# Edge softmax of a graph layer: keys loaded earlier, run marks made ahead of the scores, carries applied by two operations, differences written in place

## The chip, the cores and the metric

One core of a Trainium2 chip runs one program. The metric is device time in microseconds (us) of an execution, given as the median of three. Engines are named as the profile does: PE (TensorE) multiplies and transposes, PEld is its weight load, DVE (VectorE), ACT (ScalarE) and POOL (GpSimd) compute, SP (SyncE) starts transfers. POOL also starts the indirect DMAs, which gather one row for each of 128 indices. DMAs started by SP form one queue.

## What is computed

A residual block of 2500 tokens with 512 features: a graph attention over 80000 edges, a slice attention and a mixture of experts. Only the edge part matters here. For each of 8 heads, with `src` and `dst` the ends of an edge:

```python
diff = hr_dst - hr_src
score = s_src + s_dst + einsum(diff, a_dif) + einsum(abs(diff), a_abs) + einsum(hr_src * hr_dst, a_prd)
alpha = leaky_relu(score, 0.2)
m = segment_max(alpha, src)
ex = exp(alpha - m[src])
att = ex / (segment_sum(ex, src)[src] + 1e-16)
out = segment_sum(att * h_e[dst], src)
```

## The kernel before

The edges are sorted by source, padded, and cut into 336 groups of two tiles of 128 edges (5376 edges to a piece, 16 pieces). `program` (L1887) runs phase after phase; each phase is a block, and no engine enters the next one before all have left the last. The phases around the change are these.

`score_edges` (L970). For each group POOL gathers 2 tiles of target rows (520 floats a row) into one of six buffers `rows_v` (L1047). PE expands the source rows with a one-hot matrix into `ps_u` (L1111), which has a single buffer and so serves the two tiles of a group in turn. DVE subtracts (`w<-rows_v,ps_u`, L1073), PE transposes `w` (L1126), ACT takes magnitudes and slopes (L1157, L1164), DVE multiplies them (L1086), PE adds over the features of a head and adds a term read from `w` itself (L1135, L1138), ACT copies the scores out (L1170) and SP writes them to DRAM in four parts (L1031). The semaphore `differed` counts subtracted tiles, `summed` counts groups through L1138. The order on each engine is written out by `in_turns`: in step n an engine does each of its operations for group n minus a fixed distance, the first 12 and the last steps unrolled, the others in a loop with semaphore values computed in registers. PE's order in step n is expand tile 0 of n-2, one-hot of n-1, heads of n-6, expand tile 1 of n-2, transpose n-3. DVE's is tile 0 of n-2, multiply n-5, tile 1 of n-2, one-hot of n (L1065). POOL is unrolled.

`softmax_weights` (L1175). SP loads the four parts of the scores, each 2.7 MB as 128 rows (8 heads by 16 pieces) of 5376 columns, and then the sorted records for each head in three DMAs (`keys`, L1211 to L1213). DVE makes `reset`: 0 where the source stays the same, -1e38 where a run of equal sources ends (L1229 to L1231). It adds the four parts (L1233 to L1235), applies leaky relu (L1236), and takes the maximum within each run by a scan from the left and one from the right (L1239, L1240). The ends of each piece go through DRAM to 8 rows, are scanned over the 16 pieces and come back as a carry for each row (L1216 to L1222, L1248 to L1252). Then both scans run again with the carries as start values, and the larger of the two is subtracted from `alpha`. ACT takes exp of all 5376 columns, and 42 times PE transposes 128 columns (L1273) and ACT copies them to `weights` (L1265), with two PSUM buffers in turn.

`gather_messages` (L1276). DVE zeroes `denominators` and `sums` (L1320, L1321). POOL gathers two tiles of message rows for each group into six buffers (L1313), DVE makes one-hots (L1327) and multiplies rows by weights (L1331, two SBUF inputs), PE sums (L1355, L1356), and DVE adds these sums up (L1341, L1343).

Of the kernel before, what the change touches and what calls it, by code (L numbers as in the profile page):

```python
# [14 lines left out]
P = 128  # L15
# [954 lines left out]
def score_edges(nc, a, const, edge, group_block, tab_v, parts, parts_in, scores):  # L970
# [13 lines left out]
    with ExitStack() as ctx:  # L984
# [14 lines left out]
        w, w_abs = [sb(f"w{q}", [P, GROUP, EW]) for q in range(TURN)], sbs("w_abs", [P, KF, GE])  # L999
# [22 lines left out]
        def _(sp):  # L1022
            for tile, part in ((a_abs, 3), (minus_prd, 4)):
                for h in range(HEADS):
                    sp.dma_start(tile[h * R:(h + 1) * R, :], a["L0_gnn_a"][h, part * D:(part + 1) * D].rearrange("(c r) -> r c", r=R),
                                 allow_slow_non_contiguous=True).then_inc(vectors_in, 16)
            with nc.sync.Fori(0, GROUPS // BUFS) as t:
# [10 lines left out]
        def _(pool):  # L1038
            nc.gpsimd.iota(head_i[:, :], pattern=[[1, 1]], base=0, channel_multiplier=1).then_inc(iota_set, 1)

            for n in range(GROUPS):
                q = n % TURN
                if n >= TURN:
                    pool.wait_ge(differed, (n - TURN + 1) * GROUP)
# [6 lines left out]
        def _(dve):  # L1051
# [123 lines left out]
def softmax_weights(nc, const, scores, merged, carry, weights, from_left):  # L1175
# [6 lines left out]
    with ExitStack() as ctx:  # L1182
# [6 lines left out]
        keys = sb("keys", [P, PIECE + 2], I32)  # L1189
        reset = sb("reset", [P, PIECE + 1])  # L1190
        alpha, from_right = sb("alpha", [P, PIECE]), sb("from_right", [P, PIECE])
# [5 lines left out]
        ps_t = [ctx.enter_context(nc.psum_tensor(f"ps_weight_t{h}", [P, 512], F32)) for h in range(2)]  # L1197
        keys_in, scores_in = sem("keys_in"), sem("scores_in")
# [7 lines left out]
        def _(sp):  # L1206
            for k, part in enumerate(score_parts):
                sp.dma_start(part, scores[k * HEADS:(k + 1) * HEADS, :].rearrange("h (c x) -> (h c) x", c=CHUNKS)).then_inc(scores_in, 16)
            for h in range(HEADS):
                rows = slice(h * CHUNKS, (h + 1) * CHUNKS)  # L1210
                sp.dma_start(keys[rows, 1:PIECE + 1], merged[1:1 + EP, :].rearrange("(c x) o -> c (x o)", c=CHUNKS)).then_inc(keys_in, 16)  # L1211
                sp.dma_start(keys[rows, 0:1], merged[0:EP, :].rearrange("(c x) o -> c (x o)", c=CHUNKS)[:, 0:1], allow_slow_non_contiguous=True).then_inc(keys_in, 16)
                sp.dma_start(keys[rows, PIECE + 1:PIECE + 2],  # L1213
                             merged[2:2 + EP, :].rearrange("(c x) o -> c (x o)", c=CHUNKS)[:, PIECE - 1:PIECE], allow_slow_non_contiguous=True).then_inc(keys_in, 16)
# [734 lines left out]
```

## Time and profile before

| what | us |
|---|---|
| three executions, median (lowest to highest) | 3604.73 (3603.67 to 3625.55) |
| the profiled execution | 3586.76 |
| its span, by the trace | 3584.8 |
| busy in the span: PE, DVE, POOL, ACT | 2740.9, 2248.0, 1651.8, 1448.0 |

The profile is of one execution. Times in the rows are microseconds from the start of its span; a duration ahead of the word "mean" is in ns. The clock of PE is given as a share of full speed, 0.50 being 1.2 GHz and 1.00 being 2.4 GHz. "a <-b" after idle time names what ended it. In a row of the timeline the first number is the start and the second the time to the end of the last instruction merged into it.

### The profile page before, as it was taken

To read this page: it belongs to the slowest core of one execution; us is meant where nothing else is said; L and a number is where in the kernel's file an instruction comes from. 1 tells how busy PE (TensorE), PEld (TensorE's weight loads), DVE (VectorE), ACT (ScalarE), POOL (GpSimd) and SP (SyncE) were. 2 spreads that over 40 slices of the span, in tenths; PEclk is the share of its full clock that TensorE was granted. 3 is DMA by queue.
4 is the path that set the end of the run, shared out by engine and by line. 5 is a ranking of instruction groups with operands and counts; after the bars stand their busy time and mean duration, and the time that the engine had idled before them with its cause. 6 is when DMAs were issued, how large, how long until landed. Compare 5 with 4: busy or idle time off the path is not lost. (4 is left out here: it accounts for less than half of the span.)

```text
span 3584.8 us, 65271 instructions
## 1 busy us (share of the span) xinstructions
PE 2740.9 (76%) x17311; PEld 1764.0 (49%) x17312; DVE 2248.0 (63%) x4027; ACT 1448.0 (40%) x2941; POOL 1651.8 (46%) x1562
## 2 busy tenths in 40 slices
PE   2599887989999989989991057777777777779892
PEld 2366544666666666666661034444444444477440
DVE  3667635777777777777772967777777777742111
ACT  1233315888888888888882010000000000033220
POOL 1133204444444444444440047777777777612112
PEclk9799988999999999999996579999999999959996
DMA  3012134555555555555555035666666665641124
GB/s 115 18 61 63 56 110 124 143 142 144 142 142 144 143 142 144 143 142 144 143 136 157 0 101 165 173 175 172 174 174 174 173 174 174 164 138 48 62 77 134
DMA packets 181565, 461.62 MB, mean 129 GB/s; under 512 B 50534, under 2 KB 66338, under 8 KB 180739
## 3 DMA queue, kind: packets, MB, share of 16 engines
q0 software_dynamic: 116400, 372.54, 37.2%
q1 hardware_dynamic: 55105, 83.86, 7.5%
q10 hardware_dynamic: 10002, 4.53, 0.5%
q8 instruction: 26, 0.43, 0.1%
q14 instruction: 32, 0.26, 0.0%
HBM read 413.88 MB, written 46.86 MB: 129 GB/s over the span
## 5 line engine op out<-in xcount | busy, mean ns | idle before, releaser
L1313 POOL DMA_INDIRECT rows_e<-message_rows,edge_dst x672 | 809.8, 1205 | 431.6 <-ACTq L1286 222.9
L1047 POOL DMA_INDIRECT rows_v<-target_rows,edge_dst x672 | 639.0, 951 | 684.0 <-DVE w L1073 577.1
L1355 PE MATMUL ps_sum<-messages,node_onehot 128*125 128x512 f32 x1344 | 745.9, 643 | 243.6 <-DVE messages L1331 154.9
L1073 DVE TENSOR_TENSOR w<-rows_v,ps_u 128x520 f32<-128x520 f32 x672 | 468.0, 696 | 376.1 <-issue 284.4
L1164 ACT ACTIVATE slope<-w_abs,a_abs,minus_prd 128x256 f32<-128x256 f32 x1344 | 697.8, 593 | 0.1
L1111 PE MATMUL ps_u<-edge_space,source_onehot_t 125*128 x4032 | 593.6, 280 | 133.5 <-DVE w L1073 131.0
L1331 DVE TENSOR_TENSOR messages<-rows_e,edge_space 128x1024 f32<-128x1024 f32 x336 | 411.6, 1225 | 246.9 <-DMA rows_e<-message_rows,edge_dst 246.5
L1111 PEld LDWEIGHTS ps_u<-edge_space,source_onehot_t 125*128 125x128 bf16 x4032 | 362.9, 97 | 357.8 <-issue 279.0
L1356 PEld LDWEIGHTS ps_den<-edge_space,node_onehot 128*125 128x125 f32 x1344 | 254.5, 189 | 329.3 <-issue 329.3
L1678 ACT COPY gate_t<-ps_count 128x32 f32<-128x32 f32 x1 | 0.2, 186 | 1030.6 <-PE ps_count L1611 1030.6
L1086 DVE TENSOR_TENSOR slope<-w_abs,slope 128x1024 f32<-128x1024 f32 x336 | 409.4, 1218 | 4.2 <-ACT slope L1164 4.2
L1126 PE MATMUL ps_w<-ident,w 128*128 128x128 f32 x2688 | 349.7, 273 | 0.0
L1157 ACT ACTIVATE w_abs<-ps_w 128x1024 f32<-128x1024 f32 x336 | 342.7, 1020 | 4.1 <-PE ps_w L1126 4.0
L1355 PEld LDWEIGHTS ps_sum<-messages,node_onehot 128*125 128x125 f32 x1344 | 200.6, 189 | 272.0 <-issue 153.2
L1126 PEld LDWEIGHTS ps_w<-ident,w 128*128 128x128 f32 x2688 | 305.6, 141 | 5.0 <-issue 0.2
L1341 DVE TENSOR_TENSOR edge_space<-ps_sum,edge_space 125x512 f32 x336 | 229.9, 684 | 20.2 <-PE ps_den L1356 12.1
L1135 PE MATMUL ps_heads<-slope,head_sum 128*32 128x256 f32 x2688 | 215.5, 392 | 4.8 <-ACT score L1170 4.8
L1151 ACT COPY source_onehot_t<-ps_onehot 125x256 bf16<-125x256 bf16 x336 | 125.1, 372 | 198.5 <-issue 140.4
L1356 PE MATMUL ps_den<-edge_space,node_onehot 128*125 (+1 forms) x1344 | 190.0, 214 | 0.0
L1273 PE MATMUL ps_weight_t<-ident,alpha 128*128 128x128 f32 x42 | 14.5, 448 | 176.8 <-ACT alpha L1261 174.0
L1065 DVE TENSOR_SCALAR source_onehot<-iota_row_bf,edge_local 128x125 bf16<-128x125 bf16 x672 | 139.0, 252 | 0.1
L1327 DVE TENSOR_TENSOR node_onehot<-iota_row,edge_local 128x250 f32<-128x250 f32 x336 | 138.2, 411 | 0.1
(380 smaller groups left out, 2943.9 us busy)
## 6 DMA issues: line engine op xcount, KB each, us to landing
scores<-score SPq DMA_DIRECT2D x1344, 8.0 KB
edge_space<-in_L_ffn_w_dram SPq DMA_DIRECT2D x24, 512.0 KB, 4.7
rows_v<-target_rows,edge_dst POOLq DMA_INDIRECT x672
rows_e<-message_rows,edge_dst POOLq DMA_INDIRECT x672
source_parts<-edge_space SPq DMA_DIRECT2D x20, 380.9 KB
edge_space<-source_parts SPq DMA_DIRECT2D x4, 1904.3 KB
token_rows_out<-token_y SPq DMA_DIRECT2D x27, 256.0 KB, 2.7
edge_space<-scores SPq DMA_DIRECT2D x2, 2688.0 KB, 28.2
```

What stands on the lines that cost most here:

```text
L1047: nc.gpsimd.indirect_dma_start(rows[q][:, j, :], None, tab_v, bass.IndirectOffsetOnAxis(ap=edge["dst"][:, tile:tile + 1], axis=0)).then_in ...
L1073: v.tensor_tensor(w[q][:, j, :].rearrange("p (a b) -> p a b", a=2), rows[q][:, j, :].rearrange("p (a b) -> p a b", a=2), ps_u[:, :, 0:HALF ...
L1086: v.tensor_tensor(slope[h][:, :, :], w_abs[h][:, :, :], slope[h][:, :, :], ALU.mult).then_inc(z_set, 1)
L1111: ins = nc.tensor.matmul(ps_u[:, half, 0:HALF], onehot_t[q % BUFS][:, j, :], rows_of_part, start=part == 0, stop=part == PARTS - 1)
L1126: ins = nc.tensor.transpose(ps_w[q % 2][:, c, j * P:(j + 1) * P], w[q][:, j, c * P:(c + 1) * P], ident[:, :])
L1157: sc.activation(w_abs[h][:, :, :], ps_w[q % 2][:, :, :], ACT.Abs).then_inc(abs_set, 1)
L1164: ins = sc.activation(slope[h][:, c, :], w_abs[h][:, c, :], ACT.Identity, bias=a_abs[:, c:c + 1], scale=minus_prd[:, c:c + 1])
L1313: nc.gpsimd.indirect_dma_start(rows[q][:, j, :], None, tab_e, bass.IndirectOffsetOnAxis(ap=edge["dst"][:, tile:tile + 1], axis=0)).then_in ...
L1331: v.tensor_tensor(messages[h][:, :, :].rearrange("p j (h d) -> p (j h) d", d=D), rows[q][:, :, :].rearrange("p j (h d) -> p (j h) d", d=D) ...
L1341: v.tensor_tensor(total, ps_sum[q % BUFS][:, :], total, ALU.add)
L1355: nc.tensor.matmul(ps_sum[h][:, :], onehot[h][:, j, :], messages[h][:, j, :], start=j == 0, stop=j == GROUP - 1)
L1356: ins = nc.tensor.matmul(ps_den[h][:, 0:HEADS], onehot[h][:, j, :], tile_weights[:, DS(n * GROUP + j, 1), :].rearrange("p o h -> p (o h)") ...
```

## The change

The `keys` tile is made outside the two phases, its 24 loads are issued by SP at the start of `score_edges`, and `w` becomes another name for `rows_v`: DVE writes the difference over the gathered row. So POOL waits for `summed` of the group six before instead of `differed`, and DVE's wait on `summed` in `differ` goes. In `softmax_weights` the run marks are made without waiting for scores, and two further scans over them (`in_first`, `in_last`, the latter in bf16) mark the columns that lie in the first and the last run of a piece. The parts of the scores are added one after another, each on its own semaphore. After the carries, instead of two scans, one maximum and one subtraction over the whole width, there are three operations on each of three stretches of 2048, 2048 and 1280 columns. ACT starts on the first stretch while DVE does the next. Transposes and copies go by four. The zeroing of `denominators` and `sums` moves to DVE's stream of `softmax_weights`.

```diff
-        w, w_abs = [sb(f"w{q}", [P, GROUP, EW]) for q in range(TURN)], sbs("w_abs", [P, KF, GE])
+        w, w_abs = rows, sbs("w_abs", [P, KF, GE])
@@ score_edges, sync, ahead of the loop
+            for h in range(HEADS):
+                rows_of_head = slice(h * CHUNKS, (h + 1) * CHUNKS)
+                sp.dma_start(keys[rows_of_head, 1:PIECE + 1], merged[1:1 + EP, :].rearrange("(c x) o -> c (x o)", c=CHUNKS)).then_inc(keys_in, 16)
...
@@ score_edges, gpsimd
-                    pool.wait_ge(differed, (n - TURN + 1) * GROUP)
+                    pool.wait_ge(summed, n - TURN + 1)
@@ score_edges, vector, differ
                     at_least(dve, gathered[q], turn * (16 * GROUP) + 16 * GROUP)
-                    at_least(dve, summed, n - TURN + 1)
@@ softmax_weights, vector
             dve.wait_ge(keys_in, 16 * 3 * HEADS)
+            v.memset(lowest[:, :], -BIG)
             link(v.tensor_scalar(keys[:, :], keys[:, :], KEY.bit_length() - 1, None, ALU.logical_shift_right))
             link(v.tensor_tensor(reset[:, :], keys[:, 1:PIECE + 2], keys[:, 0:PIECE + 1], ALU.not_equal))
             link(v.tensor_scalar(reset[:, :], reset[:, :], -BIG, None, ALU.mult))
-            dve.wait_ge(scores_in, 16 * KF)
...
+            floor = lowest[:, 0:1].broadcast_to([P, PIECE])
+            v.tensor_tensor_scan(in_first, reset[:, 0:PIECE], floor, 0.0, ALU.add, ALU.max)
+            link(v.tensor_tensor_scan(in_last[:, ::-1], reset[:, 1:PIECE + 1][:, ::-1], floor, 0.0, ALU.add, ALU.max))
+            v.tensor_copy(ends[:, 2:3], in_first[:, PIECE - 1:PIECE])
+            v.tensor_copy(ends[:, 3:4], in_last[:, 0:1])
+            for k in range(1, KF):
+                dve.wait_ge(scores_in[0], 16)
+                dve.wait_ge(scores_in[k], 16)
+                link(v.tensor_tensor(score_parts[0], score_parts[0], score_parts[k], ALU.add))
...
-            v.tensor_reduce(ends[:, 2:3], reset[:, 0:PIECE], AX.X, ALU.min)
-            v.tensor_reduce(ends[:, 3:4], reset[:, 1:PIECE + 1], AX.X, ALU.min).then_inc(ends_set, 1)
+            dve.sem_inc(ends_set, 1)
+            link(v.tensor_tensor(from_right[:, :], from_left[:, :], from_right[:, :], ALU.max))
             dve.wait_ge(pieces_in, 16)
...
+            v.memset(denominators[:, :, :], 0.0)
             dve.wait_ge(carry_in, 16)
-            scans(carry_p[:, 0:1], carry_p[:, 1:2])
-            link(v.tensor_tensor(from_left[:, :], from_left[:, :], from_right[:, :], ALU.max))
-            v.tensor_tensor(alpha[:, :], alpha[:, :], from_left[:, :], ALU.subtract).then_inc(shifted, 1)
+            for begin, end in stretches:
+                at = slice(begin, end)
+                link(v.scalar_tensor_tensor(from_right[:, at], in_first[:, at], carry_p[:, 0:1], from_right[:, at], ALU.add, ALU.max))
+                link(v.scalar_tensor_tensor(from_right[:, at], in_last[:, at], carry_p[:, 1:2], from_right[:, at], ALU.add, ALU.max))
+                v.tensor_tensor(alpha[:, at], alpha[:, at], from_right[:, at], ALU.subtract).then_inc(shifted, 1)
+            v.memset(sums[:, :, :], 0.0)
@@ softmax_weights, scalar
+            for n, (begin, end) in enumerate(stretches):
+                act.wait_ge(shifted, n + 1)
+                nc.scalar.activation(alpha[:, begin:end], alpha[:, begin:end], ACT.Exp).then_inc(exped, 1)
+                for b, (i, size) in enumerate(batches):
+                    if begin <= i * P < end:
+                        act.wait_ge(turned[b % 2], b // 2 + 1)
+                        for x in range(size):
+                            ins = nc.scalar.copy(weights[:, :, i + x, :], ps_t[b % 2][:, x, :].rearrange("p (h c) -> p c h", h=HEADS))
+                        ins.then_inc(kept[b % 2], 1)
@@ gather_messages, vector
-            v.memset(denominators[:, :, :], 0.0)
-            link(v.memset(sums[:, :, :], 0.0))
```

## Rows read from the trace of the kernel before

**Rows 1.** Two stretches: us, busy of each engine (instructions), PEclk, DMA share, GB/s.
```profile
1908.20:1961.10 52.90, 0.00 (x0) 0.00 (x0) 0.00 (x0) 0.00 (x0) 0.00 (x0) 0.50 0.93 261
1961.10:2096.40 135.30, 14.48 (x42) 7.60 (x42) 103.58 (x23) 14.77 (x43) 0.00 (x0) 0.50 0.00 0
```

**Rows 2.** Timeline of SP and DVE at the loads: start, us, engine, line.
```profile
1908.16 0.37 SPq L1208 DMA_DIRECT2D alpha<-scores  x1
...
1961.12 2.96 DVE L1229 TENSOR_SCALAR keys<-keys 128x5378 int32<-128x5378 int32 x1 [59.24 <-DMA keys<-sorted_records]
1964.12 5.76 DVE L1230 TENSOR_TENSOR reset<-keys 128x5377 f32<-128x5377 int32 x1
```

**Rows 3.** Timeline of DVE: scans, ends of pieces, carries.
```profile
1995.95 11.36 DVE L1239 TENSOR_TENSOR_SCAN edge_space<-reset,alpha 128x5376 f32<-128x5376 f32 x1
2007.23 11.33 DVE L1240 TENSOR_TENSOR_SCAN from_right<-reset,alpha 128x5376 f32<-128x5376 f32 x1
...
2034.05 0.18 DVE L1248 TENSOR_TENSOR_SCAN state<-pieces 8x16 f32<-8x16 f32 x1 [3.92 <-DMA pieces<-carry]
...
2039.31 11.42 DVE L1239 TENSOR_TENSOR_SCAN edge_space<-reset,carry_p,alpha 128x5376 f32<-128x5376 f32 x1 [4.67 <-DMA carry_p<-carry]
```

**Rows 4.** Groups of instructions, 2078 to 2096: count, busy us, mean ns, idle before.
```profile
L1273 PE MATMUL ps_weight_t<-ident,alpha 128*128 128x128 f32 x42 | 14.5, 448 | 176.8 <-ACT alpha L1261 174.0
L1261 ACT ACTIVATE alpha<-alpha 128x5376 f32<-128x5376 f32 x1 | 4.7, 4682 | 168.8 <-DVE alpha L1256 168.8
```

**Rows 5.** Timeline at the change of phase to `gather_messages`.
```profile
2095.53 0.48 ACT L1265 COPY edge_space<-ps_weight_t 128x128 f32<-128x128 f32 x2 [0.35 <-PE ps_weight_t L1273]
...
2096.93 0.95 POOL L1313 DMA_INDIRECT rows_e<-message_rows,edge_dst  x1 [222.86 <-ACTq L1286]
...
2098.66 8.59 DVE L1321 MEMSET edge_space<- 125x10240 f32 x1 [2.08 <-issue]
```

**Rows 6.** Stretch in which only the key loads run; columns as in rows 1.
```profile
1936.00:1958.00 22.00, 0.00 (x0) 0.00 (x0) 0.00 (x0) 0.00 (x0) 0.00 (x0) 0.50 0.95 113
```

**Rows 7.** Timeline of the loop of `score_edges`, one step and two later.
```profile
1102.08 0.70 DVE L1073 TENSOR_TENSOR w<-rows_v,ps_u 128x520 f32<-128x520 f32 x1 [0.89 <-issue]
...
1102.57 0.39 PE L1138 MATMUL ps_heads<-ident,w 128*8 128x128 f32 x4
...
1102.69 1.22 DVE L1086 TENSOR_TENSOR slope<-w_abs,slope 128x1024 f32<-128x1024 f32 x1
...
1109.85 0.69 DVE L1073 TENSOR_TENSOR w<-rows_v,ps_u 128x520 f32<-128x520 f32 x1 [0.77 <-issue]
```

**Rows 8.** Timeline of PE: eight transposes at 1.2 GHz in `score_edges`.
```profile
573.49 1.91 PE L1126 MATMUL ps_w<-ident,w 128*128 128x128 f32 x8
```

**Rows 9.** Section 5 of the page: count, busy us, mean ns, idle before.
```profile
L1313 POOL DMA_INDIRECT rows_e<-message_rows,edge_dst x672 | 809.8, 1205 | 431.6 <-ACTq L1286 222.9
```

**Rows 10.** Timeline of POOL in `gather_messages`, in three places.
```profile
2125.26 1.92 POOL L1313 DMA_INDIRECT rows_e<-message_rows,edge_dst  x1 [0.30 <-issue]
...
2502.26 0.95 POOL L1313 DMA_INDIRECT rows_e<-message_rows,edge_dst  x1 [0.30 <-issue]
...
3113.60 1.86 POOL L1313 DMA_INDIRECT rows_e<-message_rows,edge_dst  x1 [0.30 <-issue]
```

**Rows 11.** Timeline of DVE in the same three places.
```profile
2125.13 1.23 DVE L1331 TENSOR_TENSOR messages<-rows_e,edge_space 128x1024 f32<-128x1024 f32 x1
...
2129.67 1.23 DVE L1331 TENSOR_TENSOR messages<-rows_e,edge_space 128x1024 f32<-128x1024 f32 x1 [2.31 <-DMA rows_e<-message_rows,edge_dst]
...
2505.96 1.23 DVE L1331 TENSOR_TENSOR messages<-rows_e,edge_space 128x1024 f32<-128x1024 f32 x1 [0.86 <-DMA rows_e<-message_rows,edge_dst]
...
3119.78 1.23 DVE L1331 TENSOR_TENSOR messages<-rows_e,edge_space 128x1024 f32<-128x1024 f32 x1 [0.93 <-DMA rows_e<-message_rows,edge_dst]
```

**Rows 12.** Timeline of POOL and DVE in `write_result`.
```profile
3522.69 1.19 POOL L1869 DMA_INDIRECT back<-token_rows_out,token_slot  x1 [0.30 <-issue]
...
3528.75 1.29 DVE L1876 TENSOR_TENSOR x_sb<-x_sb,back 125x512 f32<-125x512 f32 x2 [1.61 <-DMA back<-token_rows_out,token_slot]
```

More of the change, by code:

```diff
@@ L967, in sort_and_project, with score_edges @@
         clear_semaphores(nc, sems)
-def score_edges(nc, a, const, edge, group_block, tab_v, parts, parts_in, scores):
+def score_edges(nc, a, const, edge, group_block, tab_v, parts, parts_in, scores, merged, keys, keys_in):
     ident, identb, row, rowb = const["ident"], const["identb"], const["row"], const["rowb"]
@@ L1172, in _, with softmax_weights @@
             in_turns(sc, TURNS, ((4, magnitudes), (1, keep_onehot), (4, slopes), (6, keep_scores)), TURN)
-def softmax_weights(nc, const, scores, merged, carry, weights, from_left):
+def softmax_weights(nc, const, scores, keys, keys_in, carry, weights, from_left, sums, denominators):
     with ExitStack() as ctx:
@@ L1207, in _ @@
             for k, part in enumerate(score_parts):
[L1208 to L1214, printed above, removed]
+                sp.dma_start(part, scores[k * HEADS:(k + 1) * HEADS, :].rearrange("h (c x) -> (h c) x", c=CHUNKS)).then_inc(scores_in[k], 16)
             sp.wait_ge(ends_set, 1)
@@ L1258, in _ @@
+            v.memset(sums[:, :, :], 0.0)
         @block.scalar
         def _(act):
-            act.wait_ge(shifted, 1)
-            nc.scalar.activation(alpha[:, :], alpha[:, :], ACT.Exp).then_inc(exped, 1)
-            for i in range(PT):
-                act.wait_ge(turned[i % 2], i // 2 + 1)
-                nc.scalar.copy(weights[:, :, i, :], ps_t[i % 2][:, 0:P].rearrange("p (h c) -> p c h", h=HEADS)).then_inc(kept[i % 2], 1)
+            for n, (begin, end) in enumerate(stretches):
[7 more added lines that the diff above has]
+                        ins.then_inc(kept[b % 2], 1)
@@ L1267, in _ @@
         @block.tensor
         def _(pe):
-            pe.wait_ge(exped, 1)
-            for i in range(PT):
-                if i >= 2:
-                    pe.wait_ge(kept[i % 2], i // 2)
-                nc.tensor.transpose(ps_t[i % 2][:, 0:P], alpha[:, i * P:(i + 1) * P], const["ident"][:, :]).then_inc(turned[i % 2], 1)
+            for b, (i, size) in enumerate(batches):
+                pe.wait_ge(exped, i // STRETCH + 1)
+                if b >= 2:
+                    pe.wait_ge(kept[b % 2], b // 2)
+                for x in range(size):
+                    ins = nc.tensor.transpose(ps_t[b % 2][:, x, :], alpha[:, (i + x) * P:(i + x + 1) * P], const["ident"][:, :])
+                ins.then_inc(turned[b % 2], 1)
@@ L1916, in program @@
         sums = sums_space[0:L, :].rearrange("p (b f) -> p b f", b=NB)
-        score_edges(nc, a, const, edge, group_block, tab_v, parts, parts_in, scores)
-        softmax_weights(nc, const, scores, merged, carry, weights, sums_space[:, 0:PIECE])
+        keys_in = sem("keys_in")
+        with nc.sbuf_tensor("keys", [P, PIECE + 2], I32) as keys:
+            score_edges(nc, a, const, edge, group_block, tab_v, parts, parts_in, scores, merged, keys, keys_in)
+            softmax_weights(nc, const, scores, keys, keys_in, carry, weights, sums_space[:, 0:PIECE], sums, denominators)
         gather_messages(nc, const, edge, group_block, weights, tab_e, sums, denominators)
```

28 lines of the change are left out of this document (16 added, 12 removed).

## The prediction

> **What bounds the kernel now.** I read the busy time by stage first. Between the scores and the message gathers the kernel has 188 us in which no two engines work at a time. For 52.9 us no engine computes and the DMA engines are 0.93 busy; for the next 135.3 us they are still, and DVE is busy for 103.6 us [rows 1]. The timeline says what is late there. SP issues its 28 loads from 1908.16 on and DVE starts at 1961.12, when the keys have landed [rows 2]. Then DVE does one full-width operation after another, with two waits for carries of 3.92 and 4.67 us [rows 3]. Last come 4.7 us of exp and 42 transposes [rows 4]. The last copy ends at 2096.01, so the stretch from the first load takes 187.9 us. Everything in it is on the path, since no engine enters a phase before all have left the last. That is the stretch the change rewrites; the loop of the scores, which it also touches, must be looked at for harm.
>
> **Softmax stretch after the change, from 1908.2.** Full-width operations keep their measured times; the start-to-start distance is 0.03 us more than the duration where DVE waits for itself [rows 2].
>
> Marks: the keys are in SBUF long before, so DVE can start at once. I add 1.0 us for code that may not be there yet (bounds 0 and 2.08, the unexplained idle of DVE at the next change of phase [rows 5]). Two operations of 2.96 (L1229, and L1231 of the same size), one of 5.76 [rows 2], the two new scans at the price of those there (11.3 and 11.4 [rows 3]) and small ones: 34.7 us, to 1943.9. A bf16 output has no row here; I take the price of f32 and see no reason for more. The scores are 10.75 MB and land by about 1936, the key traffic alone being what follows [rows 6]. So these marks hide the score loads and the adds wait for nothing.
>
> Scores: three adds and leaky relu, four times 5.79, then two scans and two copies, 22.9: 46.1 us, to 1990.0. The two reductions over the full width are gone.
>
> Carries: DVE does the maximum, 5.8 us, while the ends travel (3.92 [rows 3]), so that wait is hidden and the maximum shows: 1995.8. The small scans take 0.6, the way back 4.67 [rows 3]: 2001.1.
>
> Stretches: a line through DVE's 1.22 us for 1024 columns [rows 7] and 5.76 for 5376 [rows 2] gives 2.29 us for 2048 and 1.49 for 1280. Nine operations: 6.9 + 6.9 + 4.5 = 18.3 us, with `shifted` at 2008.0, 2014.9 and 2019.4. Zeroing `sums` follows, 8.6 us [rows 5], and ends at 2028.0.
>
> ACT and PE: exp of 2048 columns is 4.68 x 2048 / 5376 = 1.8 to 1.9 us [rows 4]. A transpose now comes every 0.41 us, because each waits for a copy [rows 4]. In fours, back to back, it is 1.91 / 8 = 0.24 us at the same 1.2 GHz [rows 8], and four copies are some 0.9 us (0.48 for two [rows 5]). With two buffers that makes 1.1 us for four and 5.4 us for a stretch of 16. ACT: 2008.0 + 1.9 + 5.5 = 2015.4, + 1.9 + 5.5 = 2022.8, + 1.2 + 3.6 = 2027.6. If the cadence stays 0.41 it ends at 2032. So the stretch ends at 2028.0, a gain of 68 us; 64 at the slow cadence, 69 without the 1.0 us.
>
> **Gathers after it.** POOL starts 0.9 us into the phase in both [rows 5]. The 8.6 us of zeroing are worth little there: POOL sets the pace of this phase, (809.8 + 431.6 - 222.9) / 336 = 3.03 us a group [rows 9], and had all that time been gathering ahead. DVE's first product can come 0.95 + 0.30 + 0.95 + 2.8 = 5.0 us after POOL's start instead of 10.7; I take 2 us of these 5.7 (bounds 0 and 6).
>
> **Score loop: gathers released later.** POOL's gather of group n waited for the subtraction of n-6, in step n-4, and now waits for L1138 of n-6, in step n, while DVE needs the rows in step n+2. The product of the wait is a window. L1138 ends at 1102.96; the subtraction two steps on starts at 1109.85 [rows 7], 6.9 us later. Needed: 0.3 to wake, two gathers of 0.95 with 0.30 between, and the landing. For the landing I take `gather_messages`, the same 128 rows of about 2 KB: POOL ends its second gather at 2503.21 and DVE, waiting for just that, starts at 2505.96, 2.75 us [rows 10, 11]. 310 groups of that phase wait for a landing; the first of them shows 2129.67 - 2127.18 = 2.49, the last 3119.78 - 3115.46 = 4.32, and by my reading half lie under 2.73 and all but a few under 3.4. That makes a need of 5.3 us. Added to it: the first gather would now start at 1103.25, under the multiply, which runs to 1103.91 [rows 7]. In `gather_messages` a gather that starts at 2125.26, under a product from 2125.13 to 2126.35, takes 1.92 instead of 0.95 and ends 0.83 after the product [rows 10, 11]. So it ends at 1104.73 and the need is 5.8 to 5.9 us: about 1.0 us are left over and the later release costs nothing. What hides it is that window; every microsecond of landing beyond it is paid once in three steps (release, gather, subtraction, next L1138 run over three), 0.33 us x 324 = 108 us.
>
> The Trainium skill ("SBUF — State Buffer", section "SBUF: two separate sides") speaks against this change here: a DVE operation with two SBUF inputs and a GpSimd operation that reads SBUF share a port pair as an exclusive lock, and the second to start blocks until the first ends. By that rule the first gather waits under the multiply, as the 1.92 us row has it; without it the window would have 1.7 us to spare instead of 1.0. The trace agrees with the rule for the product; for this multiply no row shows it.
>
> DVE loses one wait in the subtraction, with its register operations. DVE is idle 0.77 to 0.89 before that subtraction [rows 7] and the wait lies inside that time, so I take nothing. No row prices one wait; as the far bound I take a tenth of that idle time, 0.08 us, in 324 steps: 26 us.
>
> **Keys at the start of the scores.** 24 issues, each some 0.4 us like the first score load [rows 2], end near 570 and SP's first score write comes at 587, so SP's queue is free. The loads hold the DMA engines at 0.95 for 22 us at 113 GB/s [rows 6], beside the first twelve gathers. Groups are needed only every 4 us and are gathered over 10 us ahead. I take 1 us, bounds 0 and 11 (half of 22).
>
> **Sum.** 68 + 2 - 1 = 69 us. Against the profiled execution: 3586.8 - 69 = 3517.8. The median of the runs lies 18 us above that execution: 3604.7 - 69 = 3535.7, say 3536.
>
> **Rivals.**
> *The gathers come late* (slower). Landing in the score loop is longer than where I read it. In `write_result` POOL ends a gather at 3523.88 and DVE starts at 3528.75, 4.87 us [rows 12]; there it competes with SP's writes, as it would here with score writes of 32 KB a group. Against: the phase with the same rows shows 2.75, and score writes are few. At 4.87 the excess is 4.87 - 2.75 - 1.0 = 1.1 us, 1.1 x 108 = 119 us: 3655. It outweighs the gain from a landing of 2.75 + 1.0 + 69 / 108 = 4.4 us on. Chance 0.08, and 0.04 for a landing of about 4.0, which costs 27 us: 3563.
> *The wait on DVE was on the path.* For it: that idle time is put to issue, not to PE [rows 7]. Against: its length. 3536 - 26 = 3510. Chance 0.06.
> *Keys crowd the first gathers.* For it: the engines are nearly full with them. Against: the lead of the gathers. 3546. Chance 0.10.
> *The overlap gives nothing*, ACT and PE keep their cadence and start stalls for code: 3536 + 4 + 1 = 3541. Chance 0.12.
> The forecast itself: 0.55, with its own range 3526 to 3548; some 0.05 is left for drift between runs (they span 22 us).
>
> **Numbers.** 3536, range 3515 to 3563. One per cent, 36 us, is about what a measurement of this kernel can tell from no change. Faster by more than that means below 3568.7: all cases but the late landing at its dearer end and part of the drift, 0.88. Within 1%: a landing near 4.4, 0.06. Slower: 0.06.
>
> **What would show it.** DVE starts the marks within 3 us of SP's first score load and shows no wait for scores; softmax from first load to last copy or zeroing 120 us (124 at most); the message phase unchanged at 3.03 us a group. In the score loop POOL's first gather of a pair takes longer than 0.95, and DVE does not wait for `rows_v`; a step stays at 3.95 us. I am wrong if a step grows, if DVE's idle before the subtraction is put to the DMA, or if the span to the first score load moves by more than 10 us.

## The result, and the profile after

| | before | after |
|---|---|---|
| executions | 4 | 4 |
| median us (lowest to highest) | 3613.85 (3603.67 to 3625.55) | 3441.64 (3426.19 to 3460.44) |
| ratio, 95% interval | | 0.9525 (0.9452 to 0.9598) |
| profiled execution | 3586.76 | 3456.42 |

The kernel gained 172 us where 69 were forecast: the time lies far below the range (3515 to 3563). By phase, each cut at the starts of instructions: "scores" from POOL's first gather to SP's first score load, "softmax" to POOL's first message gather, "messages" to the last product of message rows.

| profiled execution | scores | softmax | messages | rest | mean score step |
|---|---|---|---|---|---|
| before | 1356.3 | 188.8 | 1022.9 | 465.0 | 3.95 |
| after | 1255.3 | 122.3 | 1053.1 | 471.5 | 3.63 |

The softmax stretch gained 66.5 us, as worked out. The scores gained 101.0, which no term of the sum had. The messages lost 30.2, the phases after them 6.5 and those ahead of the scores 0.5. That makes the 130.3 between the two profiled executions; before's lay 18 to 27 us under the median of its runs and after's 15 above, hence 172 between the medians.

The softmax stretch of after, cut at the end of the marks, of the two scans and at POOL's first gather (us, busy of each engine with its instructions, PEclk, DMA share, GB/s), which answers to [rows 1]:

```profile
1807.60:1842.30 34.70, 0.00 (x0) 0.00 (x0) 34.44 (x9) 0.00 (x0) 0.00 (x0) 0.50 0.76 317
1842.30:1888.40 46.10, 0.00 (x0) 0.00 (x0) 45.82 (x10) 0.00 (x0) 0.00 (x0) 0.50 0.00 0
1888.40:1929.90 41.50, 9.18 (x42) 6.91 (x42) 33.90 (x18) 12.96 (x45) 0.00 (x0) 0.58 0.01 1
```

DVE is busy for 114.2 of 122.3 us: the stretch is now one engine's work. Its timeline (start, us, engine, line):

```profile
1807.72 2.96 DVE L1235 TENSOR_SCALAR keys<-keys 128x5378 int32<-128x5378 int32 x1
...
1830.78 11.33 DVE L1240 TENSOR_TENSOR_SCAN in_last<-reset,lowest 128x5376 bf16<-128x5376 f32 x1
...
1842.28 5.75 DVE L1246 TENSOR_TENSOR alpha<-alpha,from_right 128x5376 f32<-128x5376 f32 x1
...
1888.45 5.76 DVE L1253 TENSOR_TENSOR from_right<-edge_space,from_right 128x5376 f32<-128x5376 f32 x1 [0.16 <-DVE ends L1251]
...
1899.71 2.35 DVE L1264 SCALAR_TENSOR_TENSOR from_right<-keys,carry_p,from_right 128x2048 f32<-128x2048 f32 x1 [4.71 <-DMA carry_p<-carry]
...
1916.84 1.49 DVE L1266 TENSOR_TENSOR alpha<-alpha,from_right 128x1280 f32<-128x1280 f32 x1
1920.41 8.59 DVE L1267 MEMSET edge_space<- 125x10240 f32 x1 [2.08 <-issue]
...
1934.85 1.22 DVE L1344 TENSOR_TENSOR messages<-rows_e,edge_space 128x1024 f32<-128x1024 f32 x1 [5.12 <-DMA rows_e<-message_rows,edge_dst]
```

DVE starts 0.07 us after SP's first load and never waits for a score part; the wait for the pieces is covered by the maximum (L1253), and what stays is the way of the carries, 4.71, as in [rows 3]. ACT's exps and its last copies, and POOL's first gather:

```profile
1906.81 1.91 ACT L1273 ACTIVATE alpha<-alpha 128x2048 f32<-128x2048 f32 x1 [102.48 <-DVE alpha L1266]
...
1920.20 1.35 ACT L1273 ACTIVATE alpha<-alpha 128x1280 f32<-128x1280 f32 x1
1922.30 2.05 ACT L1278 COPY edge_space<-ps_weight_t 128x128 f32<-128x128 f32 x10 [0.75 <-PE ps_weight_t L1288]
...
1929.91 0.94 POOL L1329 DMA_INDIRECT rows_e<-message_rows,edge_dst  x1 [142.80 <-ACTq L1302]
```

ACT ends at 1924.35, DVE's zeroing at 1929.00 and sets the end. Now the score loop, one step of after (DVE and POOL), which answers to [rows 7]:

```profile
1100.93 1.22 DVE L1092 TENSOR_TENSOR slope<-w_abs,slope 128x1024 f32<-128x1024 f32 x1
1102.06 0.69 DVE L1079 TENSOR_TENSOR rows_v<-rows_v,ps_u 128x520 f32<-128x520 f32 x1
...
1101.50 1.46 POOL L1054 DMA_INDIRECT rows_v<-target_rows,edge_dst  x1 [0.87 <-PE ps_heads L1144]
1103.27 0.94 POOL L1054 DMA_INDIRECT rows_v<-target_rows,edge_dst  x1 [0.30 <-issue]
```

And the rows of before that I had in hand and did not put beside each other, around the multiply at 1102.69 of [rows 7]; in brackets stands the idle time ahead of an operation and what the profile says ended it:

```profile
1101.14 0.95 POOL L1047 DMA_INDIRECT rows_v<-target_rows,edge_dst  x1 [1.78 <-DVE w L1073]
1102.39 0.94 POOL L1047 DMA_INDIRECT rows_v<-target_rows,edge_dst  x1 [0.30 <-issue]
...
1104.12 0.70 DVE L1073 TENSOR_TENSOR w<-rows_v,ps_u 128x520 f32<-128x520 f32 x1 [0.21 <-PE ps_u L1111]
```

In after the second subtraction starts at 1102.06, 0.09 before the multiply's recorded end (1100.93 + 1.22 = 1102.15). In before it starts at 1104.12, 0.21 after that end (1103.91), and the second gather of the pair had begun 0.30 us ahead of the multiply. Over the loop the gap from the multiply's end to the next subtraction is +0.22 us in before and -0.08 in after; the other distances of the chain are nearly the same (first subtraction to multiply 0.61 in both, second subtraction to the next first one 1.90 and 1.88). So 0.30 us a step, times 324 steps, 97 us of the 101, sits in that one gap. Each multiply's record reads 1.22 us in either kernel.

### The profile page after: what moved, and what is told of

It reads as the page before. It is cut to its first block and busy times, and to the rows that moved or that the text cites. A ratio compares the mean times of both kernels' runs of the same rounds, so it can differ in the third digit from the quotient of the medians.

```text
span 3454.5 us, 65133 instructions
## 1 busy us (share of the span) xinstructions
PE 2751.6 (80%) x17311; PEld 1771.4 (51%) x17312; DVE 2219.3 (64%) x4036; ACT 1443.4 (42%) x2943; POOL 1809.3 (52%) x1562
## 5 line engine op out<-in xcount | busy, mean ns | idle before, releaser
L1054 POOL DMA_INDIRECT rows_v<-target_rows,edge_dst x672 | 802.5, 1194 | 433.0 <-PE ps_heads L1144 328.4
L1368 PE MATMUL ps_sum<-messages,node_onehot 128*125 128x512 f32 x1344 | 764.0, 659 | 267.4 <-DVE messages L1344 140.9
L1079 DVE TENSOR_TENSOR rows_v<-rows_v,ps_u 128x520 f32<-128x520 f32 x672 | 466.1, 694 | 300.5 <-PE ps_u L1117 288.3
L1132 PE MATMUL ps_w<-ident,rows_v 128*128 128x128 f32 x2688 | 349.7, 273 | 0.0
L1132 PEld LDWEIGHTS ps_w<-ident,rows_v 128*128 128x128 f32 x2688 | 305.5, 141 | 5.1 <-issue 0.2
L1354 DVE TENSOR_TENSOR edge_space<-ps_sum,edge_space 125x512 f32 x336 | 230.1, 685 | 91.7 <-remote 45.8
L349 POOL TENSOR_TENSOR squares<-row_v 125x512 f32<-125x512 f32 x20 | 20.9, 1045 | 228.5 <-ACT row_v L908 228.5
```

The source lines that it names most:

```text
L1054: nc.gpsimd.indirect_dma_start(rows[q][:, j, :], None, tab_v, bass.IndirectOffsetOnAxis(ap=edge["dst"][:, tile:tile + 1], axis=0)).then_in ...
L1079: v.tensor_tensor(w[q][:, j, :].rearrange("p (a b) -> p a b", a=2), rows[q][:, j, :].rearrange("p (a b) -> p a b", a=2), ps_u[:, :, 0:HALF ...
L1132: ins = nc.tensor.transpose(ps_w[q % 2][:, c, j * P:(j + 1) * P], w[q][:, j, c * P:(c + 1) * P], ident[:, :])
L1354: v.tensor_tensor(total, ps_sum[q % BUFS][:, :], total, ALU.add)
L1368: nc.tensor.matmul(ps_sum[h][:, :], onehot[h][:, j, :], messages[h][:, j, :], start=j == 0, stop=j == GROUP - 1)
```

## The experiments

In the tables and texts "step" is the mean distance of the first subtractions over 300 steps, "gap" that from the multiply's recorded end to the second subtraction, "lead" that from the second gather's start to the multiply's start. Kernels named b are the kernel before with one edit, those named a the changed kernel.

**Which of the two edits of the loop did it.** Three kernels of before and one of after.

```diff
  b_late, b_late_nowait (POOL)
-                    pool.wait_ge(differed, (n - TURN + 1) * GROUP)
+                    pool.wait_ge(summed, n - TURN + 1)
  b_nowait, b_late_nowait (DVE, differ); a_wait puts this line back into the changed kernel
-                    at_least(dve, summed, n - TURN + 1)
```

> The kernel before, with only DVE's wait on `summed` ahead of the first subtraction of a group taken out (PE's own order keeps the buffer safe). Theory W (the wait with its register operations held DVE's stream in the loop): the step of the score loop falls from 3.95 us to about 3.63 and the phase from 1356 us to about 1250. Theory G (gathers released early collide with DVE's two-input multiply or with the descriptors' writing, and the later release cured it): the step stays at 3.95. Theory P (writing in place is quicker for DVE): stays at 3.95.

> The kernel before, with only POOL's wait changed from `differed` to `summed`: gathers are released four steps later, DVE's wait and the separate `w` stay. Theory G: the step falls from 3.95 us to about 3.63. Theory W: it stays at 3.95. Theory P: it stays at 3.95. All: the first gather of a pair takes about 1.4 us instead of 0.95.

> The kernel before with both edits: POOL waits for `summed` and DVE's wait is out; `w` stays separate. Theory W and theory G: step 3.63 us. Theory P: 3.95 us.

> The changed kernel with DVE's wait on `summed` put back ahead of the first subtraction, where it is always met already. Theory W: the step returns from 3.63 to 3.95 us and the score phase from 1255 to about 1356 us. Theories G and P: it stays at 3.63 us. The softmax stretch stays at 122 us in all.

| kernel | median us | ratio to before (95%) | scores | step | gap |
|---|---|---|---|---|---|
| before, beside them | 3605.28 | | | | |
| b_nowait | 3609.35 | 1.0015 (0.9991 to 1.0040) | 1365.9 | 3.98 | +0.27 |
| b_late | 3512.66 | 0.9746 (0.9706 to 0.9787) | 1259.4 | 3.65 | -0.08 |
| b_late_nowait | 3490.66 | 0.9685 (0.9646 to 0.9724) | 1252.5 | 3.63 | -0.08 |
| a_wait | 3442.91 | 0.9553 (0.9515 to 0.9590) | 1263.2 | 3.65 | -0.08 |

The later release alone brings the whole of it (93 us in the median, 97 to 107 in the phase), the removed wait alone nothing. Beside the later release that wait is worth 0.02 us a step, some 6 us (3.65 against 3.63 in both pairs). The medians of b_late and b_late_nowait lie 22 us apart, of two executions each; of the 18.5 us between their profiled executions only 6.9 lie in the scores.

**Is it the lead or the place in the step?** The release half a step later, a whole step later, the second gather alone held back, and a kernel that leaves out the gathers from the seventh group on (its later scores are of the wrong rows).

```diff
  b_rel1
+                    pool.wait_ge(differed, (n - TURN + 1) * GROUP + 1)
  b_rel2
+                    pool.wait_ge(differed, (n - TURN + 2) * GROUP)
  b_split, in addition to the old wait
+                    if n >= TURN and j == 1:
+                        pool.wait_ge(differed, (n - TURN + 1) * GROUP + 1)
  b_nogather
+                if n >= TURN:
+                    continue
```

> The kernel before, with the release of POOL's gathers moved by half a step only: to the first subtraction of the next group (`differed` + 1) instead of the second of its own. The lead stays at five and a half steps. Theory PH (what counts is where in the step the gathers of a pair run: a second gather that runs just ahead of and under the multiply makes the subtraction behind the multiply start 0.3 us late): the gap between multiply and second subtraction falls from +0.23 to -0.08 us and the step from 3.95 to 3.64 us. Theory LD (what counts is how far ahead gathers are, or how many are in flight): the step stays at 3.95 us.

> The kernel before, with POOL's release moved by a whole step: to the second subtraction of the next group, so the same place in the step with one step less of lead. Theory PH: the step stays at 3.95 us and the gap at +0.23. Theory LD: part of the gain of the later release is seen, a step of 3.95 minus about a quarter of 0.32, 3.87 us.

> The kernel before, with only the second gather of each pair held back, to the first subtraction of the next group; the first gather stays where it was. Theory PH in its first form (the second gather, beside first subtraction and multiply, is the culprit): the step falls to 3.64 us. Its second form (the first gather, whose rows move while the multiply runs, is the culprit): the step stays near 3.95 us.

> The kernel before without its gathers of target rows from the seventh group on (buffers keep the rows of the first six groups, so later scores are of the wrong rows). It shows the step of the loop without any gather. Theories PH and LD: 3.6 us, with the gap between multiply and second subtraction at -0.08 us. If the gap stays at +0.23 us, the gathers had nothing to do with it and the delay is of DVE's own stream.

Before took 3605.82 us beside them. b_rel1: 3505.29, ratio 0.9716 (0.9628 to 0.9804), scores 1258.1, step 3.65, gap -0.08. b_rel2: 3605.67 (one execution), scores 1368.4, step 3.99, gap +0.26. b_split: 3517.3 (one), step 3.68, gap -0.05. b_nogather: 3519.93 (one), scores 1263.8, step 3.67, gap -0.08. The timelines of b_rel1 and, below it, b_rel2, one step each (POOL, then DVE):

```profile
1102.25 1.69 POOL L1047 DMA_INDIRECT rows_v<-target_rows,edge_dst  x1 [0.69 <-DVE w L1073]
...
1101.90 1.22 DVE L1086 TENSOR_TENSOR slope<-w_abs,slope 128x1024 f32<-128x1024 f32 x1
1103.04 0.69 DVE L1073 TENSOR_TENSOR w<-rows_v,ps_u 128x520 f32<-128x520 f32 x1
```

```profile
1102.84 0.94 POOL L1047 DMA_INDIRECT rows_v<-target_rows,edge_dst  x1 [0.30 <-issue]
...
1103.15 1.22 DVE L1086 TENSOR_TENSOR slope<-w_abs,slope 128x1024 f32<-128x1024 f32 x1
1104.66 0.69 DVE L1073 TENSOR_TENSOR w<-rows_v,ps_u 128x520 f32<-128x520 f32 x1 [0.29 <-PE ps_u L1111]
```

Half a step later, the first gather begins under the multiply and waits for it (1.69 us instead of 0.95, off the path). A whole step later the second gather is again 0.31 ahead of the multiply, and the 0.3 us are back. So what counts is where the gather falls in the step, not how early the rows are there. Without gathers the step is the short one (3.67): the later release speeds nothing up, it takes a loss away. b_split was not the clean case it was meant to be: its pairs slipped until a gather began under the multiply, so it agrees and decides nothing.

**A shift on POOL alone**, without touching what it waits for: two small memsets ahead of the second gather.

```diff
  b_pad
+                    if n >= TURN and j == 1:
+                        pad_link(nc.gpsimd.memset(pad[:, :], 0.0))
+                        pad_link(nc.gpsimd.memset(pad[:, :], 0.0))
  b_inplace: b_late_nowait, and
-        w, w_abs = [sb(f"w{q}", [P, GROUP, EW]) for q in range(TURN)], sbs("w_abs", [P, KF, GE])
+        w, w_abs = rows, sbs("w_abs", [P, KF, GE])
```

> The kernel before with two tiny memsets on POOL, each waited for, between the two gathers of a pair: more work, the same release. They move the start of the second gather from 0.2 us ahead of the multiply's start to behind it. Theory LK (a lock between the two: a gather that starts first holds the multiply's second input for 0.5 us, which shows only as a late subtraction; one that starts under the multiply waits for its end): the gap behind the multiply falls from +0.23 to -0.08 us, the second gather takes up to 1.8 us, the step falls to about 3.65 us, the score phase to about 1260 us. Rival MV (the moving rows or the descriptors' writing of the first gather slow the subtraction): the first gather is where it was, so the gap and the step of 3.95 us stay.

> The kernel before with the score loop of the changed one: POOL waits for `summed`, DVE's wait is out, `w` is `rows_v`. The softmax phase and the key loads are those of before. If writing in place is worth nothing, step 3.63 us and score phase 1253 us, as with a separate `w`. Against it the changed kernel should show the softmax part by itself: 66 us less, all in the softmax stretch (188 us here), and 3 us more in the score phase for the key loads.

b_pad took 3509.44, ratio 0.9752 (0.9701 to 0.9804), step 3.68, and the second gather mostly starts after the multiply does and waits under it (mean 1.76 us): two memsets that move the gather by 0.26 us are worth 93 us there. (Steps with it still 0.02 to 0.08 ahead are few, twelve, and they have a gap of +0.11 to +0.20.) b_inplace took 3489.0, scores 1253.4 against 1252.5 of b_late_nowait: writing the difference over the row is worth nothing in itself; it is what makes the later release needed. Against after (1255.3) it also prices the key loads at the start: some 2 us, from one execution of each.

**Towards a faster kernel.** The products of the message phase cut into two of 128x512, so that POOL gets in between (a_half); and half of `sums` zeroed in the wait for the carries (a_best has both, a_zero this alone).

```diff
  a_half, gather_messages
-                w = tile_weights[:, DS(n * GROUP, GROUP), :].rearrange("p j h -> p (j h)")
...
+                for j in range(GROUP):
+                    w = tile_weights[:, DS(n * GROUP + j, 1), :].rearrange("p j h -> p (j h)")
...
  a_best, a_zero, softmax_weights
+            v.memset(sums[:, 0:NB // 2, :], 0.0)
             dve.wait_ge(carry_in, 16)
...
-            v.memset(sums[:, :, :], 0.0)
+            v.memset(sums[:, NB // 2:NB, :], 0.0)
```

> The changed kernel with the product of `gather_messages` made in two halves of 512 columns, both after both rows have landed. By theory LK each half holds off a gather for 0.68 us at most instead of 1.22, and the gather gets in between: POOL's pace falls from 3.02 us a group to 2.75 or less and the message phase from 1025 to about 930 us. If the lock is no more than a correlation there, DVE does 0.09 us more in a group, the pace stays at 3.02, and the total stays within 10 us of the changed kernel's.

> The same with half of `sums` zeroed while DVE waits for the carries (4.7 us idle), the other half behind the last stretch. The softmax stretch should end with ACT's last copy instead of the zeroing: 118 us instead of 122, and the total 4 us below that of the kernel with the two halves alone.

a_half took 3485.10 and a_best 3480.93 us, both about 40 above the changed kernel (3441.64; a_wait took 3442.91 on the same chip as they). POOL did run ahead: the median distance of two products is 2.34 us in a_half and 2.97 in after. But the message phase took 1069.9 and 1057.9 us instead of the 930 expected, since DVE stood still again and again: 37 and 36 times the next product came more than 5 us after the last, where before has three such distances and after 14. In after a stall looks like this in the timeline, and the waits of DVE (us in total, times, longest) put 45.8 us to `remote`:

```profile
2037.18 1.24 DVE L1344 TENSOR_TENSOR messages<-rows_e,edge_space 128x1024 f32<-128x1024 f32 x1 [0.26 <-issue]
2048.63 0.69 DVE L1354 TENSOR_TENSOR edge_space<-ps_sum,edge_space 125x512 f32 x1 [10.20 <-remote]
```

```profile
DVE edge_space L1354 <- remote: 45.8, 7, 11.5
```

The same in a_half:

```profile
DVE edge_space L1356 <- remote: 105.1, 21, 10.7
```

`remote` is only the profile's name for a releaser that it didn't find. The stall is DVE's own: in 2037.2 to 2045.7 its sequencer, the part that issues its instructions and works out addresses and semaphore values, takes 0.69 to 0.73 us for each of seven instructions in front of the addition. The line that does this work for the additions (count, then shortest, median and longest duration in ns), in after and, below it, in a_again, the same kernel in a later execution without stalls:

```profile
L1350 DVEq FUSED_REGOPS  x660: 2/190/724, 1941.4 to 2985.6; - x165
```

```profile
L1350 DVEq FUSED_REGOPS  x660: 53/190/210, 1939.6 to 2946.2; - x165
```

Of DVE's 2400 register instructions in the message phase 72 took over 0.4 us in after, some in each of its fifteen stalls of over 2 us, and 95 of 2726 in a_half; in the whole phase of a_again there is none. Why the sequencer is slow there is open. The next two kernels asked whether the stalls belong to the program.

> The changed kernel once more, beside the next one. Theory (the hold of the multiply is gone, the softmax stretch is 66 us shorter): score step 3.63 to 3.65 us, scores 1255 to 1263, softmax 122, total 3426 to 3460 as in its other runs. The message phase decides where in that span it lies: if the stalls of DVE every 16 groups belong to the program, messages is near 1053 again with some 14 stalls over 5 us; if they vary from execution to execution, it is 1022 to 1032 with few.

> The changed kernel with half of sums zeroed while DVE waits for the carries, the other half after the stretches; the products of the message phase stay whole. Theory: softmax 118 to 119 us instead of 122.3 (as with halved products, 118.7), and the message phase, paced by POOL at 3.03 us a group, gives nothing back: total 3 to 4 us below the run beside it. Rival: the phase start is set by something else, or message stalls of DVE (up to 30 us) swamp it: no difference that can be told, or either sign.

They do not: the same changed kernel now had no distance over 5 us, messages 1014.6, and took 3422.77 (3410.06 to 3428.34). a_zero took 3419.63 (3418.95 to 3426.79), softmax 118.7 instead of 122.3: the stretch is 3.6 us shorter as expected and the median 3.1 lower, which lies within the scatter of the runs: the lowest median of all, but not shown to be faster. The surprise was the kernel before, run beside them: **3488.53 us** (3475.38 to 3493.21, 7 runs), and so a ratio of 0.9821 (0.9780 to 0.9862), a gain of 66 us instead of 172. The chip was another one, chip 11 instead of 9.

**The kernel before on other chips.** The kernel before unedited, twice, on chips 5 and 12, and once with one memset ahead of the first gather of each pair (b_pad0: as b_pad, with `j == 0` and one memset).

> The kernel before once more, with its trace. Beside the last two kernels it took 3488.5 us, 117 us less than in the other calls, and the changed kernel only 19 less. Theory (the second gather of a pair starts just ahead of the multiply and holds it): an execution near 3490 has a score step near 3.65, a gap of -0.08 us from the multiply's end to the second subtraction, and gathers that start after the multiply does, or far enough ahead of it; one near 3605 has 3.95 and +0.23. Rival: the 117 us lie elsewhere (softmax, messages, experts), and the score step is 3.95 at either time.

> The kernel before, once more with its trace. If its time is near 3605, the score step is 3.95 to 4.0 us, the second gather starts 0.29 us ahead of the multiply and the second subtraction 0.22 to 0.26 after its end, as in the two traces of it so far. If its time is near 3490, as beside the last two variants of the changed kernel, the step is 3.65 and the gather starts after the multiply; a step of 3.95 at 3490 would be against the theory of the hold.

> The kernel before with one small memset on POOL ahead of the first gather of each pair, so that both gathers start some 0.2 to 0.3 us later in the step. The second starts 0.29 ahead of the multiply in the kernel before. Theory of the hold, with its border where the gather meets the start of the multiply: in many or all steps the gather now starts with or after the multiply and waits itself (1.7 to 1.9 us), step 3.65 to 3.8, total 3490 to 3560. Rival, that the later start counts only by several tenths more: 3605.

| kernel, chip | us | scores | softmax | messages | step | lead | gap |
|---|---|---|---|---|---|---|---|
| before, first trace | 3586.76 | 1356.3 | 188.8 | 1022.9 | 3.95 | 0.29 | +0.22 |
| b_again, chip 5 | 3609.61 | 1366.9 | 188.8 | 1029.2 | 3.99 | 0.29 | +0.25 |
| b_again2, chip 12 | 3492.21 | 1256.0 | 188.4 | 1020.0 | 3.65 | 0.29 | -0.08 |
| b_pad0, chip 12 | 3492.95 | 1255.2 | 188.1 | 1022.2 | 3.65 | 0.05 | -0.08 |
| after, first trace | 3456.42 | 1255.3 | 122.3 | 1053.1 | 3.63 | | -0.08 |
| a_again, chip 11 | 3418.47 | 1256.1 | 122.3 | 1014.6 | 3.63 | | -0.08 |

One step of b_again2 (POOL, then DVE) and its busy times in 560 to 1800:

```profile
1099.47 0.94 POOL L1047 DMA_INDIRECT rows_v<-target_rows,edge_dst  x1 [1.51 <-DVE w L1073]
1100.71 0.95 POOL L1047 DMA_INDIRECT rows_v<-target_rows,edge_dst  x1 [0.30 <-issue]
...
1100.99 1.22 DVE L1086 TENSOR_TENSOR slope<-w_abs,slope 128x1024 f32<-128x1024 f32 x1
1102.13 0.69 DVE L1073 TENSOR_TENSOR w<-rows_v,ps_u 128x520 f32<-128x520 f32 x1
```

```profile
560.00:1800.00 1240.00, 1201.25 (x11398) 852.19 (x11400) 931.69 (x1680) 1178.48 (x2345) 632.17 (x667) 0.99 0.57 153
```

The same stretch in the first trace of before:

```profile
560.00:1800.00 1240.00, 1112.59 (x10551) 788.21 (x10552) 888.50 (x1560) 1091.93 (x2170) 596.09 (x628) 0.99 0.52 143
```

The gather stands exactly where it stood, 0.28 us ahead of the multiply, and the second subtraction follows without the 0.3, which the theory of the hold had not allowed for: it wanted the gather elsewhere in an execution near 3490. The whole difference between the two executions, b_again and b_again2, is 117.4 us, and 110.9 of it lie in the scores. In every trace of before that took 3585 to 3625 us the delay is there (before, b_again, and b_nowait and b_rel2 with their edits); on chip 12 it is absent, and the median of before on chip 11, 3488.5, fits its absence, though no trace of before was taken there. Chips 4, 5, 11 and 12 were used at one time each and chip 9 at two, with medians of before of 3605 and 3602 us; so the chip is the likely difference, and that it is the chip and not the moment isn't shown. b_pad0 fell on chip 12 as well, where there was no delay to cure; it shows only that a mean lead of 0.05 does no harm there either.

**What comes late.** The expectations speak of a hold of the multiply by the gather. The traces also keep the times of the semaphore updates, the signals with which one engine lets another go on (some are missing in them), and these say something else. The multiply's own signal, where it is recorded, comes 0.01 us after its recorded end in every trace, with the delay and without. The second subtraction waits for PE's expansion of the second tile, as the brackets above say. PE's row stands 0.81 us after the first subtraction in before and, below it, in b_again2:

```profile
1102.89 0.84 PE L1111 MATMUL ps_u<-edge_space,source_onehot_t 125*128 x6
```

```profile
1101.19 0.84 PE L1111 MATMUL ps_u<-edge_space,source_onehot_t 125*128 x6
```

But its signal comes later (medians of 300 steps, us; PE's recorded ends are modelled):

| trace | expansion's recorded end to its signal | signal to second subtraction | recorded end to signal of L1138 |
|---|---|---|---|
| before | 0.36 | 0.02 | 1.05 |
| b_again | 0.39 | 0.02 | 1.09 |
| b_nowait | 0.40 | 0.02 | 1.09 |
| b_rel2 | 0.40 | 0.02 | 1.09 |
| b_again2 | 0.01 | 0.08 | 0.02 |
| b_rel1 | 0.01 | 0.08 | 0.02 |
| b_nogather | 0.01 | 0.08 | 0.02 |
| a_again | 0.01 | 0.06 | 0.02 |

In the four traces with the delay the subtraction starts 0.022 to 0.024 us after PE's signal, step after step, and 0.38 to 0.42 after the expansion's recorded end; in the other fifteen the median is 0.07 to 0.10 after that end (seven of them lack nearly all of these signals). So the lost time is a wait for PE's signal, and nothing shows the multiply held. L1138, PE's last product of a group, ends under the second gather in the four; but in after the expansion of the first tile ends 0.6 us into a gather with its signal on time, so that alone isn't enough. What keeps PE's signals back is open: it takes the gathers (b_nogather) in their old place (b_rel1, b_late, b_pad), and no run took the multiply away to see whether it has a part in it.

## Why the prediction was right or wrong

**Softmax, 68 forecast, 66.5 measured.** Marks 34.6 us (34.7), adds, relu and scans 46.1 (46.1), maximum to the first stretch 11.3 (11.1), the stretches 18.6 (18.3). DVE started at once, so the 1.0 us for code was not needed. Instead the idle of 2.08 us ahead of the zeroing [rows 5] came along with the zeroing, wherever it stands: 1916.84 + 1.49 = 1918.33, and L1267 starts at 1920.41. I had read that idle as belonging to the change of phase; it belongs to that memset. In a_zero, where the memset is cut in two, each half has half of it:

```profile
1895.08 4.33 DVE L1261 MEMSET edge_space<- 125x5120 f32 x1 [1.01 <-issue]
...
1918.83 4.33 DVE L1268 MEMSET edge_space<- 125x5120 f32 x1 [1.01 <-issue]
```

The price to put into the sum was 10.7 us, not 8.6. ACT was done 116.7 us after the first load (119.4 in the sum; a transpose took 0.23 us in fours) and stayed hidden. The bf16 output cost what f32 does (11.33).

**Messages, 2 forecast.** The first product came 4.94 us after POOL's first gather (5.0). What that is worth can't be read out of executions that scatter from 1015 to 1033 us and, with the stalls, to 1053. The 30 us that the first trace of after lost there are no effect of the change: the same kernel took 1014.6 in another execution.

**Keys at the start, 1 forecast**, some 2 measured.

**The removed wait, 0 forecast**: 0.02 us a step, 6 us, where the delay is gone; nothing where it is there. The rival's 26 us were a far bound, four times too much.

**The later release, 0 forecast: this is the step that failed.** It measured a gain of 93 us in b_late. Its working held in what it priced. The window was wide enough: DVE's first subtraction waits for PE, and for rows in only seven of 336 groups, 9.7 us in all, the longest 3.31 at 591.04. The first gather does wait under the multiply, 1.46 us instead of 0.95, and ends 0.81 after it (1101.50 + 1.46 against 1102.15). On the page of the profile its mean over the phase rises from 951 to 1194 ns, and POOL has that time (433.0 us idle):

```profile
L1054 POOL DMA_INDIRECT rows_v<-target_rows,edge_dst x672 | 802.5, 1194 | 433.0 <-PE ps_heads L1144 328.4
```

The 108 us that I had ready for a landing too late never came into it. What failed is the sentence "costs nothing" read as "moves nothing": it took the step of 3.95 as the work's own. I asked what POOL would wait for after the change, and not what its gathers did to the step before it. The multiply's record, 1.22 us long, was untouched, and the 0.21 of idle time in front of the second subtraction was put to PE, whose expansion had a recorded end at 1103.73, 0.39 earlier. That was right: PE's signal came at 1104.10. The distance stood in the rows, 324 times. The tail of before, where no gathers are left, shows it within the same trace: step 3.65 and the second subtraction at 1878.46, 0.09 ahead of the multiply's end at 1878.55.

```profile
1877.33 1.22 DVE L1086 TENSOR_TENSOR slope<-w_abs,slope 128x1024 f32<-128x1024 f32 x1
1878.46 0.69 DVE L1073 TENSOR_TENSOR w<-rows_v,ps_u 128x520 f32<-128x520 f32 x1
```

The Trainium skill ("SBUF — State Buffer", section "SBUF: two separate sides"), which I cited, has the lock in both directions: whichever starts first keeps the pair for its whole instruction. I used half of the rule, and that half held: the first gather waits under the multiply. By the other half the multiply would be held until the second gather's end, some 0.65 us. The traces of before show a delay of 0.30, of another operation, with the multiply's signal on time, and none on chip 12; so they don't bear that half out for this pair of operations.

**And the forecast's size.** On chip 11 the gain was 66 us between the medians, against 69 in the sum. There the sum stands as it was worked out, but for small terms that cancel (softmax 1.5 less, keys 1 more, the wait 6 that it had at nothing), and in part that is luck. It lacked the loss of some 100 us in the score loop that some executions of before have and others don't, and the median that it started from had it. The first result also has the stalls in after's messages against it.

## What to carry to other kernels

When the profile puts a wait to an engine whose recorded end lies some tenths of a us earlier (0.39 here, against 0.1 elsewhere), take it seriously: the signal can be late though no record is longer. Compare the distance with a stretch of the same loop in which POOL is idle. Here the cure was order, not speed: released later (half a step is enough, b_rel1), POOL's gather starts under the multiply and waits there, where POOL has slack. And time before and after on more than one chip before a gain is quoted: here it was 172 us in one place and 66 on chip 11.

## What the runs showed of the hardware

- PE's signals can come late with no record showing it: 0.36 to 0.40 us (expansion) and 1.05 to 1.09 (L1138) after the recorded end in before, b_again, b_nowait and b_rel2, against 0.01 and 0.02 in b_again2, b_rel1, b_nogather and a_again.
- Where it is there, the delay goes with the second gather's start: over 293 steps of before, gap = 0.50 - 0.97 x lead (correlation -0.78), and in b_again 0.54 - 0.96 x lead (-0.79). So the second subtraction starts some 1.73 us (1.77) after the gather does, with a scatter of 0.05. In twelve steps of b_pad with leads of 0.02 to 0.08 it is 1.41 to 1.47, so the rule is one of this place in the step. On chip 12, 294 steps of the same program with the same leads (0.03 to 0.36) have no gap above -0.04. Why is open.
- A gather that starts under the multiply waits: in the score loop of after it takes 1.45 us on average instead of 0.95 and ends some 0.8 after the multiply. The same is seen in every trace of the message phase, on each of the chips (mean of a gather 1.13 to 1.21 us).
- With the delay gone ACT is nearly the limit of the score loop: busy 1178.5 of 1240 us (0.95) against 1091.9 (0.88), and the shortest step is 3.52.
- DVE's stalls in the message phase (up to 11.5 us idle) vary: no distance of two products over 5 us in the four traces from chips 11 and 12, 0 to 14 in the others with whole products, 37 and 36 with halved ones. In them DVE's sequencer takes some 0.70 us for instructions that otherwise take 0.06 to 0.2, while POOL and the DMAs go on (2038 to 2048 in after: POOL busy 7.56 of 10 us, DMA 0.72). Why is open.
- The idle that DVE shows ahead of a large memset goes with its size, 2.08 us for 10240 columns and 1.01 for 5120, about a quarter of the recorded duration in both: by these rows it is part of what the memset costs.
